# Row maxima of an attention kernel: from two 128-row products in spare banks to two 64-row products in the score ring, with the exponentials written to SBUF

## The reference

```python
h = _group_norm(x, gn_w, gn_b)
qkv = jnp.einsum('oc,bcn->bon', qkv_w, h.reshape(B, C, N)) + qkv_b[None, :, None]
q, k, v = ...                       # (8, 8 heads, 64, 1024) each
attn = jnp.einsum('bhdi,bhdj->bhij', q, k) * HEAD_DIM ** (-0.5)
attn = jax.nn.softmax(attn, axis=-1)
out = jnp.einsum('bhij,bhdj->bhdi', attn, v)
out = jnp.einsum('oc,bcn->bon', proj_w, out.reshape(B, C, N)) + proj_b[None, :, None]
x = x + out.reshape(B, C, H, W)
```

## Time and profile before

| | |
|---|---|
| median of 3 runs | 2719.96 us |
| lowest and highest | 2717.45 and 2722.62 us |
| span of the profiled execution (its own time; no other time of it is given) | 2718.4 us |
| TensorE busy | 2619.7 us, 96% |
| VectorE busy | 2055.1 us, 76% |
| ScalarE busy | 1578.5 us, 58% |
| first to last score tile | 49.1 to 2209.9 us |

### The profile page before, as it was taken

The page is one execution under the profiler, slowest core; times in us unless marked ns, Lnnn a source line. Parts: engine busy times, 40 slices in busy tenths (PEclk is TensorE's granted clock), DMA queues, the critical chain, the costliest instruction groups (busy, mean ns, idle before and its releaser), DMA issues.

```text
span 2718.4 us, 33180 instructions
## 1 busy us (share of the span) xinstructions
PE 2619.7 (96%) x11856; PEld 2181.7 (80%) x11856; DVE 2055.1 (76%) x3294; ACT 1578.5 (58%) x1930; POOL 221.9 (8%) x134
## 2 busy tenths in 40 slices
PE   6999999999999999999999999999999987899998
PEld 5788888888888888888888888888888876688887
DVE  6788768876887688768876887688767867878864
ACT  4667646764676467646764676567646663334311
POOL 1000000000000000000000000000000012111010
PEclk9999999999999999999999999999999999899999
DMA  4512232223222322232223222321322335466444
GB/s 156 177 50 80 67 103 61 79 71 100 64 78 67 101 67 76 63 107 67 65 72 109 66 59 79 109 67 48 90 83 58 112 127 203 171 215 246 165 164 170
DMA packets 154849, 279.48 MB, mean 103 GB/s; under 512 B 51776, under 2 KB 52032, under 8 KB 154176
## 3 DMA queue, kind: packets, MB, share of 16 engines
q1 hardware_dynamic: 152128, 268.98, 31.4%
q0 software_dynamic: 2560, 8.39, 1.0%
HBM read 180.04 MB, written 63.18 MB: 89 GB/s over the span
## 4 chain that ended last, share of the span: by engine, by line
PE 83%; DVE 9%; issue 3%; DMA 2%; ACT 1%; SPq 0%; POOL 0%; POOLq 0%; DVEq 0%; ACTq 0%
PE tiles L372 9%; PE tiles L373 8%; PE tiles L374 8%; PE tiles L474 8%; PE tiles L451 8%; PE tiles L428 8%; PE tiles L468 8%; PE tiles L467 8%; PE tiles L447 7%; PE tiles L1321 5%; PE tiles L1371 2%; DVE row_max L679 2%; DVE p_low L695 2%; DVE h_low L787 1%; PE tiles L383 1%
## 5 line engine op out<-in xcount | busy, mean ns | idle before, releaser
L679 DVE TENSOR_REDUCE row_max<-tiles 128x1 f32<-128x512 f32 x1014 | 694.5, 685 | 443.4 <-PE tiles L428 440.6
L544 ACT ACTIVATE p_high<-tiles 128x1024 fp32r<-128x1024 f32 x512 | 525.5, 1026 | 595.8 <-PE tiles L451 595.1
L695 DVE TENSOR_TENSOR p_low<-tiles,p_high 128x1024 fp32r<-128x1024 f32 x512 | 623.0, 1217 | 7.0 <-ACT tiles L546 6.2
L546 ACT ACTIVATE tiles<-tiles 128x1024 f32<-128x1024 f32 x512 | 523.0, 1021 | 0.0
L467 PE MATMUL tiles<-p_high,v_high 128*128 128x512 f32 x1024 | 406.5, 397 | 2.2 <-ACT num_den L562 1.5
L428 PE MATMUL tiles<-k_high_low,q_high_high 128*128 128x512 f32 x1014 | 404.8, 399 | 0.2 <-DVE row_max L679 0.2
L468 PE MATMUL tiles<-p_high,v_low 128*128 128x512 f32 x1024 | 402.0, 393 | 0.0
L428 PEld LDWEIGHTS tiles<-k_high_low,q_high_high 128*128 128x128 f32 x1014 | 312.5, 308 | 48.6 <-DVE row_max L679 5.7
L474 PE MATMUL tiles<-p_low,v_high 128*128 128x512 f32 x1024 | 325.8, 400 | 14.9 <-DVE p_low L695 14.6
L451 PE MATMUL tiles<-q_low_max,k_high_one 65*128 65x512 f32 x1024 | 325.8, 399 | 1.9 <-DMA q_low_max<-row_max_top 1.8
L372 PE MATMUL tiles<-h_high,w_high 128*128 128x512 f32 x768 | 304.6, 397 | 17.3 <-DVE row_max L679 8.3
(11 more groups left out here) (167 smaller groups left out, 3138.1 us busy)
## 6 DMA issues: line engine op xcount, KB each, us to landing
x_tiles<-in_x SPq DMA_DIRECT2D x64, 512.0 KB, 5.4
w_high<-w_split SPq DMA_DIRECT2D x126, 256.0 KB, 2.8
w_low<-w_split SPq DMA_DIRECT2D x126, 256.0 KB, 3.0
k_high_one<-k_high_low SPq DMA_DIRECT2D x128, 128.0 KB, 2.3
q_high_high<-q_high_high SPq DMA_DIRECT2D x128, 128.0 KB, 2.3
o_normed<-rec_rows SPq DMA_DIRECT2D x64, 256.0 KB, 3.7
x<-x_tiles SPq DMA_DIRECT2D x32, 512.0 KB, 4.0
x_full<-x SPq DMA_DIRECT2D x32, 512.0 KB, 8.3
```

What stands on the lines that cost most here:

```text
L544: nc.scalar.activation(ph[:, r, :], ring[:, r, :], ACT.Exp, scale=ATT_SCALE).then_inc(s_ph, 1)
L546: nc.scalar.activation(ring[:, r, :], ring[:, r, :], ACT.Exp, scale=ATT_SCALE).then_inc(s_p32, 1)
L679: nc.vector.reduce_max(mcol[:, h % 2, n, i:i + 1], max_bank(h, i, n)[:, :], AX_X).then_inc(s_mx, 1)
L695: tt(pl[:, r, :], ring[:, r, :], ph[:, r, :].bitcast(F32), ALU.subtract).then_inc(s_pl, 1)
```

## The change

- `max_products`: a block's two products have K = 64 and 512 keys each. The first uses rows 0 to 63 (high parts in `q1[0:64]`, `k1[0:64]`), the second rows 64 to 127 (their copies in `q1[64:128]`, `k2[64:128]`). They are issued together behind the scores; k's low part no longer enters the maximum.
- Both go to the ring slot that the next step's scores will use. So the products wait until the last tile's exponentials are done, and the next scores wait until the maximum has been taken.
- One `reduce_max` of 1024 columns a block, behind the low parts of the projections; `top_of_halves` and its column pairs are gone.
- The full exponentials go to `p_full` in SBUF, and `scores` waits for them and no longer for `p_low`. `p_low` reads both its operands from SBUF.
- `k_high_one` and `q_low_max` change their halves, and L451's products take 128 rows, of which 63 are zero; GpSimd sets these at the start.
- The plan of the banks has projections alone.

```diff
-READ_BEHIND = dict(m=8, k=26, q=26, v=12, vt=28, o=26, g=22)
+READ_BEHIND = dict(k=26, q=26, v=12, vt=28, o=26, g=22)
...
+        def max_products(h, i, out):
+            first = (i // 4) * HALF + i % 4
+            queries = slice(first, first + HALF - 3, 4)
+            mm(out[:, 0:HALF], q1[0:HD, q_slot(h), queries], k1[0:HD, k_slot(h), 0:HALF], start=True, stop=True)
+            mm(out[:, HALF:N], q1[HD:P, q_slot(h), queries], k2[HD:P, k_slot(h), HALF:N], start=True, stop=True
+               ).then_inc(s_max, 1)
...
-        def take_max(h, i, n):
+        def take_max(h, i, t):
             g = h // 2
             if h % 2 == 0 and i == 0:
-                pe.wait_ge(s_kql, kq(("k", g, n)))
+                pe.wait_ge(s_kqh, kq(("k", g, 1)))
+                pe.wait_ge(s_twin["k", 1], 32 * (g + 1))
...
-            fill_free(("m", h, i, n))
-            first = (i // 4) * HALF + i % 4
-            mm(max_bank(h, i, n)[:, :], q1[:, q_slot(h), first:first + HALF - 3:4], k1[:, k_slot(h), n * HALF:(n + 1) * HALF],
-               start=True, stop=True).then_inc(s_max, 1)
+            if t > 0:
+                pe.wait_ge(s_p32, t)
+            else:
+                pe.wait_ge(s_mx, maxima(0, NT - AHEAD - 1))
+            max_products(h, i, ring[:, (t + 1) % 2, :])
 
         def scores(h, s):
             t, wk, wq = h * STEPS + s, k_slot(h), q_slot(h)
             if t > 1:
-                pe.wait_ge(s_pl, t - 1)
-            else:
-                pe.wait_ge(s_mx, 2 * (NT - AHEAD))
+                pe.wait_ge(s_p32, t - 1)
+            behind = max_tile(*before(h, s)) if t > 0 else (0, NT - AHEAD - 1)
+            if behind:
+                pe.wait_ge(s_mx, maxima(*behind))
...
-                last = mm(out[:, n * HALF:(n + 1) * HALF], k2[0:HD + 1, wk, keys[n]], q2[0:HD + 1, wq, queries],
+                last = mm(out[:, n * HALF:(n + 1) * HALF], k2[:, wk, keys[n]], q2[:, wq, queries],
...
             if block:
-                take_max(*block, 0)
+                take_max(*block, t)
             for u, parts in PARTS.get((h, s), []):
                 unit_work(u, parts)
             if t > 0:
                 weigh_high(t - 1)
-            if block:
-                take_max(*block, 1)
...
-            nc.scalar.activation(ring[:, r, :], ring[:, r, :], ACT.Exp, scale=ATT_SCALE).then_inc(s_p32, 1)
+            if t > 1:
+                act.wait_ge(s_pl, t - 1)
+            nc.scalar.activation(p_full[:, r, :], ring[:, r, :], ACT.Exp, scale=ATT_SCALE).then_inc(s_p32, 1)
...
-            tt(mtop[:, h % 2, blocks], mcol[:, h % 2, 0, blocks], mcol[:, h % 2, 1, blocks], ALU.max
-               ).then_inc(s_mtop, 1)
+            nc.vector.reduce_max(mtop[:, h % 2, i:i + 1], ring[:, (t + 1) % 2, :], AX_X).then_inc(s_mx, 1)
...
-            tt(pl[:, r, :], ring[:, r, :], ph[:, r, :].bitcast(F32), ALU.subtract).then_inc(s_pl, 1)
+            tt(pl[:, r, :], p_full[:, r, :], ph[:, r, :].bitcast(F32), ALU.subtract).then_inc(s_pl, 1)
...
             if t > 0:
-                behind = before(h, s)
-                done = max_tile(*behind)
-                if done:
-                    reduce_max(*done, 1)
-                    if done[1] % 4 == 3:
-                        top_of_halves(done[0], done[1] // 4)
                 p_low(t - 1)
+                for u in UNITS.get(before(h, s), []):
+                    unit_low(u)
             if block:
-                reduce_max(*block, 0)
-            if t > 0:
-                for u in UNITS.get(behind, []):
-                    unit_low(u)
+                reduce_max(*block, t)
...
-        nc.gpsimd.memset(k2[HD:HD + 1, :, :].bitcast(F32), -1.0).then_inc(s_pset, 1)
+        nc.gpsimd.memset(q2[0:HD, :, :].bitcast(F32), 0.0).then_inc(s_pset, 1)
         pool.wait_ge(s_pset, 3)
+        nc.gpsimd.memset(k2[0:HD, :, :].bitcast(F32), 0.0).then_inc(s_pset, 1)
+        pool.wait_ge(s_pset, 4)
+        nc.gpsimd.memset(k2[0:1, :, :].bitcast(F32), -1.0).then_inc(s_pset, 1)
+        pool.wait_ge(s_pset, 5)
```

More of the change, by code:

```diff
@@ L141, with take @@
 BANKS = 3
-READ_BEHIND = dict(m=8, k=26, q=26, v=12, vt=28, o=26, g=22)
+READ_BEHIND = dict(k=26, q=26, v=12, vt=28, o=26, g=22)
 def bank_events():
     events, at, last = [], 0, {}
-    def take(e, closed=None):
+    def take(e):
         if e not in last:
-            events.append((e, closed))
+            events.append(e)
         last[e] = at
@@ L160, in bank_events @@
         for s in range(STEPS):
-            block = max_tile(h, s)
-            at += 7
-            if block:
-                take(("m", *block, 0), before(h, s))
+            at += 8
             for u, parts in PARTS.get((h, s), []):
@@ L168, in bank_events @@
                 take(u)
-            at += 5
-            if block:
-                take(("m", *block, 1))
+            at += 4
     for u in EPILOGUE:
@@ L181, in assign_banks @@
     until, holder, bank, had = [0] * BANKS, [None] * BANKS, {}, {}
-    for e, closed in events:
-        open_banks = [i for i in range(BANKS) if closed is None or holder[i] not in UNITS.get(closed, [])]
-        i = min(open_banks, key=lambda i: until[i])
+    for e in events:
+        i = min(range(BANKS), key=lambda i: until[i])
         bank[e], had[e] = i, holder[i]
@@ L235, in attention_layer @@
     pl = sb("p_low", [P, 2, N], F32R)
-    sb("spare", [P, 2, N])
+    p_full = sb("p_full", [P, 2, N])
     nd = sb("num_den", [P, 2, N])
@@ L306, in fill_of, with maxima @@
         return banks[BANK[u]]
-    def max_bank(h, i, n):
-        return banks[BANK["m", h, i, n]]
+    def maxima(h, i):
+        return h * NT + i + 1
     h32 = Count([(0, 0)] + [(b, t) for b in range(1, BATCH) for t in range(CT)])
@@ L403, in unit_work, with take_first_max @@
                 project(u, parts)
-        def take_first_max(i, n):
-            if n == 0 and i % 4 == 0:
+        def max_products(h, i, out):
[4 more added lines that the diff above has]
+               ).then_inc(s_max, 1)
+        def take_first_max(i):
+            if i % 4 == 0:
                 pe.wait_ge(s_kqh, kq(("q", 0, i // 4)))
                 pe.wait_ge(s_twin["q", i // 4], 32)
[L410 to L413, removed]
-            first = (i // 4) * HALF + i % 4
-            mm(ring[:, i % 2, n * HALF:(n + 1) * HALF], q1[:, 0, first:first + HALF - 3:4],
-               k1[:, 0, n * HALF:(n + 1) * HALF], start=True, stop=True).then_inc(s_max, 1)
-        def take_max(h, i, n):
+                pe.wait_ge(s_kqh, kq(("k", 0, 1)))
+                pe.wait_ge(s_twin["k", 1], 32)
+            if i > 1:
+                pe.wait_ge(s_mx, i - 1)
+            max_products(0, i, ring[:, i % 2, :])
+        def take_max(h, i, t):
             g = h // 2
             if h % 2 == 0 and i == 0:
-                pe.wait_ge(s_kql, kq(("k", g, n)))
+                pe.wait_ge(s_kqh, kq(("k", g, 1)))
+                pe.wait_ge(s_twin["k", 1], 32 * (g + 1))
             if h % 2 == 0 and i % 4 == 0:
@@ L497, in tensor @@
                 for i in range(4):
-                    for n in range(2):
-                        take_first_max(i, n)
+                    take_first_max(i)
             if u == ("v", 0, 1):
-                for n in range(2):
-                    take_first_max(4, n)
-        pe.wait_ge(s_pset, 3)
+                take_first_max(4)
+        pe.wait_ge(s_pset, 5)
         for h in range(ALL_HEADS):
@@ L665, in split_low, with reduce_first_max @@
             tt(low, raw, high.bitcast(F32), ALU.subtract).then_inc(s_rawl, 1)
[L667 to L670, removed]
+        def reduce_first_max(i):
+            dve.wait_ge(s_max, i + 1)
+            nc.vector.reduce_max(mtop[:, 0, i:i + 1], ring[:, i % 2, :], AX_X).then_inc(s_mx, 1)
         def normed_first(t):
@@ L705, in kq_low @@
                 w = q_slot(h) if kind == "q" else k_slot(h)
-                to = q2[0:HD] if kind == "q" else k1[HD:P]
+                to = q2[HD:P] if kind == "q" else k1[HD:P]
                 high = q1[0:HD] if kind == "q" else k1[0:HD]
@@ L851, in vector @@
             unit_low(u)
[L852 to L857, removed]
+        for i in range(5):
+            reduce_first_max(i)
         for u in PROLOGUE[6:]:
```

34 lines of the change are left out of this document (12 added, 22 removed).

## The result

The changed kernel takes 2841.02 us (median of 4 runs, 2835.90 to 2842.79) against 2721.15 for the kernel before beside it (4 runs): a ratio of 1.0441, 95% interval 1.0428 to 1.0453. It is slower by 120 us, where 70 us less were forecast; the time lies between the two prices of rival 1.

What follows compares the result with a forecast made beforehand. TensorE's number of matmuls was taken as the bound. From the profiled 2718.4 us, -79 - 6 + 10 + 5 = -70 gave 2648, 2650 as median; 2625 to 2695 with uncertain waits, whole range 2620 to 2830.

Steps and rivals of the forecast that it cites:

- rival 1: TensorE, changing to half rows and back empties the array; 2773 us, about 2985 if loads can't run ahead; chance 0.25.
- the first term of the change: TensorE's block products: two taking 0.47 us become a pair of 0.27, gaining 0.20 us a step.
- What bounds the kernel: In the stretch of the score tiles, the number of matmuls on TensorE sets the time; only 27 us idle.
- that costs little now: Block products' stepped weights: a load of 0.31 us against 0.19 stays hidden behind the product before.
- The argument against rival 1: L451's products of 65 rows stand between products of 128 at the usual slots, two in 0.47 us.
- its second form: At the change of rows, loads can't run ahead either: 0.31 and 0.19 us more, 1.06 in all, about 2985 us.
- Rival 2: TensorE's halves don't run side by side, the second load waiting for the first: pair 0.47, about 2735 us; chance 0.20.
- The loop: Next scores need the reduction's slot; steps like 19.7 without projections take 3.10 us instead of 2.78, 10 us lost.
- `p_low` and GpSimd: With both operands in SBUF, p_low may be held by GpSimd's L878: 5 us for all heads, from above 112.
- The start: GpSimd sets 3072 and 4096 columns more, 6.1 us, hidden by its 7.51 us wait for VectorE: costs nothing.
- the 65 rows turned 128: L451's products on TensorE take 128 rows at the same 512 columns and 0.23 us: costs nothing.

Runs made afterwards that it cites:

- with full rows: Changed kernel with only the row halves undone (128-row products, still in the ring, exponentials to SBUF): 2707.91 us, 0.9957 of the kernel before; again 2709.58 us.
- in the order of the kernel before: Kernel before with only the full exponentials going to SBUF and p_low reading both operands from there: 2735.36 us, ratio 1.0059.
- these two runs: Changed kernel with each pair issued twice: 2945.59 us, 105 above it; changed kernel with only the row halves undone: 2707.91 us.

## Why the prediction was wrong

The step that failed is the first term of the change: "I take 0.27 for the pair: one slot, and 0.03 for two starts that don't quite coincide". The starts coincide to 3 ns and the halves do run side by side; the pair itself takes one slot. What the term left out is the way there and back, which rival 1 had: the run-out on each side and two weight loads that no longer run ahead, 0.745 us in all instead of 0.27. The Trainium skill, "TensorEngine Tiling (Array Packing)", "Key Properties", says that switching the tiling mode drains TensorE, and the trace agrees: on each side 0.09 us beyond the usual slot in which no matmul starts. The Trainium skill, "TensorE: Matmul & The Clock Gate", "Part 3: Packing small matmuls — row/col tiling", has the starts of such products some 4 ns apart, and the trace agrees with 3 ns.

Point by point:

- What bounds the kernel: right. The loss is TensorE's own time.
- "that costs little now, because the product starts 0.23 us after its load does": true of the kernel before, and the cover went with the change of rows. The stepped load is 0.225 of the 0.745, and in the sum it stood at nothing.
- The argument against rival 1, that 65 rows stand among 128 at the usual slots, didn't bear: 65 rows needed no change, 64 do.
- Rival 1 gave 0.56 or 1.06 us. The mechanism was its second form, the size between: 0.16 was put for running out from recorded durations, and 0.09 measured; 0.31 and 0.19 for the loads, and 0.225 and 0.11 measured, so a load's recorded duration is longer than the time for which it holds up its product, and a matmul's reaches further past its slot than the run-out does. By the measured terms the pairs alone come to 141 us; the row halves cost 131, since in steps without projections they take the place of waits, and the other parts gave back 11.
- Rival 2 fell: with one product instead of two the time is the same.
- The loop: right in kind and size. Step 19.7 takes 3.02 us with full rows (3.10 forecast), and 17 us are lost in steps without projections (10 forecast). That the steps with six matmuls would gain 22 us even with full rows was not forecast. In the changed kernel itself the loop hardly shows, because TensorE is later: the steps without projections lose 26 us there, 0.31 each, where those with six matmuls lose 0.22.
- `p_low` and GpSimd: right in kind; 17.6 us of VectorE's time are lost in the changed kernel, and in the order of the kernel before some 16 us of the whole time. That GpSimd's product would in turn be held by `p_low` was not forecast.
- The start and the 65 rows turned 128: L448's products take the usual 391 ns. The first score tile comes at 50.9 us instead of 49.1, but it also comes at 53.0 and 49.5 in two executions of the kernel with full rows; nothing shows beyond that.

## What to carry to other kernels

Products on half the rows should pay only when several pairs follow each other: by the times the first cost 0.73 us here (0.47 + 131/512), a further one 0.20 (105/512), against 0.47 for two full products, so two pairs in a row about break even and from three on they should gain, an estimate from these two runs. It wasn't tried: a block fills a slot of the ring, and the rest of `tiles` is in use. Before costing a matmul by its slot, ask which cover its weight load needs: a step in the weights that cost 0.01 us behind a full product cost 0.12 where nothing hid it. And when a change bundles several parts, run them apart: here one lost 131 us, and the rest together gained 11.

## What was not expected of the hardware

- A weight load read with a step of four elements holds up its product for 0.225 us where a plain one holds it for 0.11, and two such loads for different rows run at once (767.71 and 767.72, 0.30 us each).
- `p_low`, a VectorE instruction with both operands in SBUF, waits for the rest of a GpSimd product that began before it, 3.45 us instead of 1.22, and a GpSimd product waits for a `p_low` that began before it, up to 3.41 us instead of 2.40; cutting GpSimd's instruction in four brought the worst `p_low` to 1.81.
